# Attention pipeline: transposes, values and relative values one unit further behind the scores

## The reference

```python
Q, K, V = proj(Wq), proj(Wk), proj(Wv)            # 16 heads of 16
scores = einsum('bhqd,bhkd->bhqk', Q, K) / 4
scores += einsum('bhqd,qkd->bhqk', Q, pek[idx]) / 4   # idx: key minus query, clipped to +-256, plus 256
attn = softmax(where(causal, scores, -inf))
out = einsum('bhqk,bhkd->bhqd', attn, V) + einsum('bhqk,qkd->bhqd', attn, pev[idx])
x = layernorm(x + out @ Wo.T)
x = layernorm(x + silu_gated_ffn(x))              # hidden size 768, int weights times 1/127
```

## Time and profile before

| | |
|---|---|
| median of three runs | 5697.15 us |
| profiled execution, its own time | 5692.29 us |
| its span, first to last instruction | 5690.6 us |
| attention, first to last score matmul | 443.4 to 4459.9 us |
| busy over the span | TensorE 91%, VectorE 66%, ScalarE 61%, GpSimd 32% |
| mean granted TensorE clock | 0.988 |
| HBM traffic | 1417 MB in DMA packets, mean 249 GB/s |

### The profile page before, as it was taken

How to read it: one execution, slowest core, us unless ns; L and a number is a source line. 1 busy time by engine, 2 the same in 40 slices (tenths; PEclk the granted TensorE clock), 3 DMA queues, 4 the chain that set the end, 5 groups by cost and what they waited for, 6 DMA issues and landing times. The chain is left out here.

```text
span 5690.6 us, 143051 instructions
## 1 busy us (share of the span) xinstructions
PE 5152.2 (91%) x49460; PEld 3349.3 (59%) x49460; DVE 3768.7 (66%) x8777; ACT 3493.0 (61%) x7512; POOL 1837.6 (32%) x2516
## 2 busy tenths in 40 slices
PE   8977889989988889989889988998989799999999
PEld 5544556656655566566556656665665555665665
DVE  4556777777777777777777777777777555555554
ACT  4436787777777777777787777777777411111111
POOL 3443333333333333333333333333333111111111
PEclk9998999999999999999999999999999899999999
DMA  7888999999999999999999999999999411111111
GB/s 223 254 241 264 311 308 314 316 310 313 307 314 302 313 310 312 306 313 312 302 312 316 312 297 312 312 314 308 311 312 313 158 59 59 59 59 57 55 53 38
DMA packets 653784, 1417.28 MB, mean 249 GB/s; under 512 B 64004, under 2 KB 362088, under 8 KB 640872
## 3 DMA queue, kind: packets, MB, share of 16 engines
q1 hardware_dynamic: 653160, 1409.10, 77.3%
HBM read 737.46 MB, written 671.35 MB: 248 GB/s over the span
## 5 line engine op out<-in xcount | busy, mean ns | idle before, releaser
L792 ACT ACTIVATE a_prob<-a_neg_s,a_neg_max 128x384 f32<-128x384 f32 (+1 forms) x1792 | 1073.7, 599 | 261.4 <-DVE a_neg_max L841 232.9
L513 DVE COPY a_p_t<-a_t_ps 128x512 f32<-128x512 f32 (+3 forms) x1536 | 953.6, 621 | 229.5 <-PE a_t_ps L756 229.1
L689 PE MATMUL a_s_ps<-a_k,a_q 96*128 96x512 bf16 (+3 forms) x3072 | 857.7, 334 | 178.5 <-ACT a_far L796 166.2
L756 PE MATMUL a_t_ps<-a_ident,a_prob 128*128 128x128 f32 x5120 | 910.1, 278 | 78.8 <-DVE a_p_t L513 68.6
L841 DVE CUSTOM_DVE_ANT_1 a_neg_s<-a_s_ps,a_bias,a_far_neg 128x384 f32<-128x384 f32 x1280 | 791.1, 618 | 237.2 <-DVE a_far_neg L835 237.2
L835 DVE TENSOR_REDUCE a_far_neg<-a_s_ps 128x1 f32<-128x640 f32 (+4 forms) x1280 | 704.6, 550 | 302.0 <-POOL a_bias L664 176.4
L799 ACT ACTIVATE a_b_out<-a_t_ps 128x512 f32<-128x512 f32 (+1 forms) x1024 | 581.3, 568 | 369.6 <-PE a_t_ps L699 365.0
L717 PE MATMUL a_o_ps<-a_p_t,a_v 128*32 128x128 f32 x18432 | 786.2, 281 | 0.2 <-ACT a_o_t L804 0.2
L799 ACT ACTIVATE a_p_t<-a_t_ps 128x512 f32<-128x512 f32 (+3 forms) x1536 | 669.0, 436 | 137.2 <-PE a_t_ps L756 118.7
L796 ACT ACTIVATE a_far<-a_s_ps,a_neg_max 128x640 f32<-128x640 f32 (+4 forms) x1280 | 725.6, 567 | 0.0
L756 PEld LDWEIGHTS a_t_ps<-a_ident,a_prob 128*128 128x128 f32 x5120 | 607.1, 141 | 167.9 <-DVE a_p_t L513 153.0
(11 more groups left out here) (99 smaller groups left out, 6639.1 us busy)
## 6 DMA issues: line engine op xcount, KB each, us to landing
a_bias<-bias_scr SPq DMA_DIRECT2D x448, 576.0 KB, 6.4
prob_scr<-a_prob SPq DMA_DIRECT2D x448, 576.0 KB, 6.9
bias_scr<-a_b_out SPq DMA_DIRECT2D x448, 512.0 KB, 4.9
a_band<-prob_scr SPq DMA_DIRECT2D x448, 512.0 KB, 5.8
qk_scr<-p_parts SPq DMA_DIRECT2D x256, 192.0 KB, 3.4
v_scr<-p_v_out SPq DMA_DIRECT2D x256, 128.0 KB, 2.2
a_v<-v_scr SPq DMA_DIRECT2D x64, 512.0 KB, 6.9
attn_scr<-a_o_t SPq DMA_DIRECT2D x512, 64.0 KB, 6.5
```

Source lines behind the costliest of these rows:

```text
L513: copy(p_t[par][:, head, blocks[0] * P:(blocks[-1] + 1) * P], bank[:, 0:len(blocks) * P]) \
L689: mm = pe.matmul(s_ps[:, u % 2, c:e], q_s[0:ROWS, g, u, qb * P:(qb + 1) * P], k_s[0:ROWS, g, u, c:e], start=True, stop=True)
L756: mm = pe.transpose(bank[:, n * P:(n + 1) * P], prob_block(kk, head, b), ident[:, :])
L792: e = act.activation(near_prob(k, u, near(qb)), neg_s[:, u % 2, 0:w].rearrange("p (b c) -> p b c", c=P), ACT.Exp, bias=neg_max[:, u:u + 1] ...
```

## The change

Four constants change, and the code that runs `relative` and copies its result takes a lag of four tiles instead of three.

```diff
-        P_LAG = 6
-        BAND_SLOTS = ((1, 3), (2, 3))
-        VALUE_SLOTS = ((0, 3), (1, 3), (2, 3))
-        REL_SLOT = (3, 3)
+        P_LAG = 7
+        BAND_SLOTS = ((2, 3), (3, 3))
+        VALUE_SLOTS = ((1, 3), (2, 3), (3, 3))
+        REL_SLOT = (0, 4)
@@ TensorE
-                        if u == REL_SLOT[0] and ok(k - 3) and k >= 0:
-                            relative(r, k - 3)
+                        if u == REL_SLOT[0] and ok(k - 4) and k >= 0:
+                            relative(r, k - 4)
@@ ScalarE
-                        if u == REL_SLOT[0] and ok(k - 3) and k >= 0:
-                            act.wait_ge(o_mm, T - 2)
-                            if ok(k - 5):
-                                act.wait_ge(stored[(k - 3) % 2], pair(r, k - 5))
-                            act.activation(o_t[:, (k - 3) % 2], o_ps[:, 0:P], ACT.Copy).then_inc(o_evac, 1)
+                        if u == REL_SLOT[0] and ok(k - 4) and k >= 0:
+                            act.wait_ge(o_mm, T - 3)
+                            if ok(k - 6):
+                                act.wait_ge(stored[k % 2], pair(r, k - 6))
+                            act.activation(o_t[:, k % 2], o_ps[:, 0:P], ACT.Copy).then_inc(o_evac, 1)
```

## The result

The changed kernel takes 5719.18 us (median of ten runs, 5714.47 to 5725.22) against 5695.86 us of the kernel before (ten runs, 5687.10 to 5711.39). The ratio is 1.004, 95% interval 1.003 to 1.005. The forecast was 5658 us and a faster kernel; the time lies in its range, the sign is wrong.

A forecast was written before the change was run, and what follows sets the result against it. No engine plainly bound attention: TensorE bounded small steps, chained waits held large ones. Terms -1.76 + 1.2 - 1.1 + 0 + 1.1 = -0.56 us per group, times 64 is -36, plus 1, gave 5658 us; range 5560 to 5745.

The forecast's parts named there:

- Parts 1 and 2: Attention, per group: 16 transposes leave small steps for large ones, -1.76 us; VectorE's third four-block copy in large steps, +1.2.
- Part 3: Relative values, moved further behind the band's second copy, wait less for it: -1.1 us per group; values part 0 costs 0.
- Part 4, the ring: Reuse of three banks: distance three in large steps, two in small ones; 0 us per group, between -1 and +1.2.
- Part 5, the bias chain: Bias fetch to mask to maximum: work leaves that stretch, the fetch has 0.9 us less; +1.1 per group, mostly tile 7.
- Part 6: Fill and drain: one unit more once, +1 us in the whole run.
- The DMA floor: Attention's DMA engines are 96% busy, leaving at most 160 us to gain if busy share is the limit; no term used it.
- more than forecast: Rival: VectorE's added copies and the bias chain are hidden; -183 us, 5509, cut by DMA to about 5535; chance 0.12.
- nothing comes out: Rival: DMA takes all the gain, shorter small steps only make the next large tile's bias later; about 5694 us; chance 0.18.
- VectorE's rival: VectorE paces large steps, TensorE waiting at bias job 0 for a bank; +0.7 us per group, 5736 us; chance 0.21.
- The clock rival: A later bias makes the lower granted clock the rule in one group of two; +1.1 per group, 5728 us; chance 0.07.

The follow-up runs named there:

- the third buffer: Kernel before with a third bias tile buffer, its bias fetch issued earlier, ahead of the bias save: 5593.29 us; same edit on the changed kernel: 5576.06 us.
- copy before maximum: Changed kernel, but in unit 3 of small steps VectorE copies head 0 out before the next large tile's first maximum: 5828.21 us, ratio 1.024.

## Why the prediction was wrong

The sum was -0.56 us per group. Measured is +0.36 (23.3 us over 64), and the runs split it: transposes -1.40 (5503.95 less 5593.29), values, relative values and bands +1.13 (5576.06 less 5503.95), the fetch +0.63. These are differences of medians, and the split depends on the order of the moves. With the late fetch the transposes alone are worth nothing (ratio 1.0007), values and relative values on top bring 1.0014, and the bands on top of that 1.004.

**Parts 1 and 2, transposes and VectorE's copies: mechanism right, size too small, and the fetch left out.** Forecast -1.76 and +1.2, together -0.56. Measured -1.40, with the fetch out of the way, and nothing with the late fetch. The means over the groups 2 to 63, with the buffer: large steps 33.6 against 31.7, 1.9 us longer; small steps 26.1 against 29.4, 3.3 us shorter and not 1.76. Of these 3.3, unit 2 lost 2.5, more than 16 transposes at 0.11, and unit 0 lost 0.8, where the head has as many blocks as before. In unit 2 the small steps with one, two or three blocks in the second bank lost 0.69, 0.58 and 0.47 us, where three blocks should be 0.33. I have not separated this; the band job behind a short second bank waits for the second bias copy, which fits the order of the three, but no run took that wait away.

**Part 3, relative values: this is the step that failed.** Its -1.1 was the wait of the relative values for the band copy. That wait goes with the transposes alone, while the relative values still stand in unit 3. These rows are the kernel with the third buffer, then the same with `P_LAG = 7`:

```profile
PE a_o_ps L728 <- ACT a_band_t L798: 73.8, 194, 0.8
```

```profile
PE a_o_ps L728 <- ACT a_band_t L798: 1.8, 4, 0.8
```

Without the third buffer it falls from 70.1 to 1.7 in the same way. So its 1.1 per group was nothing that moving the relative values could add; what it was worth is in the -1.40 of the transposes already. And what was late next was costed at nothing. "`values` part 0 waits for the output copy; a score and a transposed head lie between as before, so 0": before, a bias job lay between as well. The row now shows 0.34 us in step 3:

```profile
2483.11 0.64 PE L729 MATMUL a_o_ps<-a_band_t,a_pv 128*32 128x128 f32 x16
2483.69 0.39 PE L689 MATMUL a_s_ps<-a_k,a_q 96*128 96x512 bf16 x1
2483.92 0.27 PE L756 MATMUL a_t_ps<-a_ident,a_wide 128*128 128x128 f32 x1
2484.53 0.42 PE L717 MATMUL a_o_ps<-a_p_t,a_v 128*32 128x128 f32 x8 [0.34 <-ACT a_o_t L804]
2485.20 0.39 PE L689 MATMUL a_s_ps<-a_k,a_q 96*128 96x512 bf16 x1 [0.25 <-ACT a_far L796]
```

The band job right behind the second bias job waits for that bias copy (49.0 us with the third buffer, 21.0 of them with the transposes alone), and head 1 of a small tile for the band copy, which the part named and left unpriced. With the third buffer, values and relative values cost 0.62 per group and the bands 0.51, where the part had -1.1 for the one and no term for the other.

**Part 4, the ring: open.** The bank wait of bias job 0 in the small steps came, 0.4 us in step 2 on average and next to nothing in the others. In the large steps, with the third buffer, 0.3 in step 6 went and 0.2 in step 7 came. What the part did not name is whose bank it is: after the change, bias job 0 of a large step takes the bank of head 0's first four blocks, which VectorE copies behind the late maximum. Before, ScalarE copied that bank, and the late maximum first held up the second bank of head 2, two jobs later. No run changed the ring alone.

**Part 5, the bias chain: right in kind, somewhat too dear, and not in its place.** Forecast +1.1, measured +0.63. It is not tile 7 in full and little of the others, but tile 5. Averaged over 17 or 18 groups, the stretch from the last scores of step 6 to the first of tile 5 fell from 10.64 to 9.10 us, while the fetch was issued 2.5 us into it instead of 2.9 and took 8.5 to the mask's end instead of 8.6. Its maximum then started 2.0 us after its scores instead of 1.1. For tiles 6 and 4 it started 0.3 and 0.1 to 0.3 us later, and for tile 7 the stretch stayed at 8.5. I had added up the work of step 4 and taken it for all. The part also did not see that the transposes of part 1 leave the same stretch. Moved alone, they shorten it by 0.3 to 0.6 us for tiles 7, 6 and 4, the fetch of tile 5 takes 0.5 longer, and VectorE's wait for the mask rises from 158.2 to 336.1.

**Part 6** is far under what these runs resolve.

**The DMA floor was no floor.** The kernel with the third buffer and moved transposes ran attention in 3825.3 us (445.3 to 4270.6), 191 us shorter than before, where the floor allowed 160, with the share at 0.98. With the rule cited from the Trainium skill's "Perfetto Trace Analysis", Identifying the Most-Contended Engine, the trace agrees: the rate rose by 5%, from 310 to 325 GB/s, as the stage got 5% shorter, while the share went from 0.96 to 0.98 and did not tell how much was to be had.

The rival "more than forecast" falls: with the mask in time, the third copies are not hidden, and the large steps are 1.9 us longer. The rival "nothing comes out" had the right mechanism for the transposes alone, with another cause: not DMA throughput but one fetch's place in a loop. VectorE's rival had the right sign and the right wait, the one before bias job 0, but the wrong reason for it: with the mask in time that wait is a quarter. The clock rival falls for the change itself, with 12 groups against 10 at the lower level; a lower clock goes with what the transposes alone lose.

## What to carry to other kernels

When a stage has a fetch that ends just as it is needed, work saved between its issue and its use is not saved: move the issue first, here with one more buffer, and then judge the schedule. Such a wait may show on another engine, at a buffer whose release is queued behind the late instruction; follow it back before calling that engine the pace. And for each wait that a move takes away, list what stands between the same pair of instructions afterwards, in each kind of step, and make sure that no other move of the same change has already taken the wait away.

## What the runs showed that I had not expected

- Transposes moved between step kinds shortened the small steps by nearly twice their count times their start-to-start time (3.3 us against 1.76).
- The DMA busy share in attention was 0.96 at 308 and 310 GB/s and 0.98 at 325, while attention got 5% shorter; a share near one did not mean that the engines were at their end.
- The granted clock went with late first maxima. Of 62 groups, 10, 12, 28 and 58 touched a stretch at 1.2 GHz in the kernel before, the changed one, the transposes alone and copy before maximum. With the third buffer it was 1 in the kernel before, 8 in the changed one, and none in the other two.
- A 576 KB fetch took 6.4 us to land beside 310 GB/s of traffic in total, and still 4.9 us beside 204 GB/s (medians).
